# Graph attention and routed experts on one core: a bound on the gathers of the edge pass, and dead edges sent beyond it

## The chip, the cores and the metric

The program runs on one NeuronCore of a Trainium2 chip. The metric is the device time of one execution in microseconds, the median of several. The engines that matter are PE (matrix products), DVE (vector), ACT (scalar functions), POOL (GpSimd, which here makes most of the indirect DMAs) and SP (plain DMAs). Each runs its own instructions in order and waits for the others through semaphores.

## The reference

6250 nodes with 256 features and 100,000 edges, sorted by destination. First a graph attention layer with 8 heads of 32, on layer-normed features, then a layer of 8 experts of which each node takes two; both are added to the residual.

```python
x_l = (x @ W_l + b_l).reshape(n, H, C)
x_r = (x @ W_r + b_r).reshape(n, H, C)
x_j = x_l[src]
g = leaky_relu(x_r[dst] + x_j, 0.2)
alpha = einsum('ehc,hc->eh', g, att) + log(edge_attr)[:, None]
ex = exp(alpha - segment_max(alpha, dst)[dst])
alpha = ex / (segment_sum(ex, dst)[dst] + 1e-16)
out = segment_sum(x_j * alpha[..., None], dst, n).reshape(n, H * C) + bias
...
h = gelu(einsum('td,edh->teh', xf, W1) + b1)
y = einsum('teh,ehd->ted', h, W2) + b2
out = einsum('ted,te->td', y, mask_of_the_two_best_experts)
```

What matters for the change is `x_l[src]`: for every edge, one row of the left table.

## The kernel before

It has four stages. `prepare` norms 49 tiles of 128 nodes and projects them (one tile after another, index `t`), writes the left rows (256 features and 8 numbers for the linear part of the score, 1056 B, the table `left_rows` of 6272 rows) and the right rows to HBM, and builds the lists of the edge pass beside that. `edges` is the edge pass. `route` normalises the sums and chooses experts; `experts` works through 105 tiles of slots, with an indirect DMA of rows in (L1267) and one with addition out (L1657) for each.

Edges are cut into 391 blocks of 256 (`PAIR` = 2 tiles of 128), and each block is worked once for every tile of 128 nodes that its destinations reach. Such a piece of 128 places is an *item*. A block in which a border between two node tiles falls is done twice, as four items instead of two. An edge whose destination lies in the other node tile is dead in that item: its `key` is -1 and its weight is nothing (`-BIG` is added to the logarithm). Each item still gathers all of its 128 left rows, those of dead edges too.

In `prepare`, the edges of the items are gathered on POOL (L332: `rows_d`, `rows_s`, `rows_w`, each with a row of 128 numbers for every item), cast by ACT into `df` (t = 21) and `sf` (t = 24), and DVE makes from them, between the projections of the tiles t = 22 to 26, `local`, `live` and `key` (L657 to L669). At this point an item is a row: partition and the index q of 7 give the item, the last index the edge. From t = 26 PE transposes `local`, `sf` and the logarithms of the weights (L476), one piece of 128 items for each tile, so that the edges lie on the partitions, and ACT copies them out (L532), the sources into `srcs` as whole numbers.

The edge pass runs over 220 groups of four items (878 items and two more). For each group, GpSimd issues four indirect DMAs (L829), one an item, each of 128 rows from `left_rows` into `rows`, by 128 source numbers out of `idx`. `rows` is a ring of 16 groups (`RINGS`): before the first gather of a group, POOL's queue waits for DVE to have weighed the group 15 before it (`weighed`), for the gathers four groups back to have landed, and for the list `idx`, which DVE copies for eight groups at once (L893). PE then sums the right rows (L1191) and the gathered rows (L1193) into `p_row`, ACT rectifies (L1081), DVE scales, adds the linear part and reduces (L909, L914, L924), after every eight groups the maxima are spread and the weights made, and eleven groups later DVE weighs the rows (L1000), PE multiplies by the one-hot destinations (L1254) and DVE adds to the accumulators (L1029). The order on each engine is fixed by the lists of stages and offsets handed to `pipeline`; no instruction order depends on data.

Of the kernel before, what the change touches and what calls it, by code (L numbers as in the profile page):

```python
# [17 lines left out]
ALU = mybir.AluOpType  # L18
# [3 lines left out]
P = 128  # L22
# [16 lines left out]
QI = -(-ITEMS // P)  # L39
# [13 lines left out]
SLOT_TILES = (2 * N + EXPERTS * (P - 1)) // P  # L53
TINY_WEIGHT = 1e-19
SPARE = 704
BY = 7
AHEAD = 8
LEAD = 7
# [4 lines left out]
SENDS = 4  # L63
BATCHES = NODE_TILES // BY
PIECES = ((0, BY), (BY, 4 * BY), (4 * BY, 7 * BY))
PARTS = ((0, 3 * BY), (3 * BY, 6 * BY), (6 * BY, 7 * BY))
EARLY = 3
DL = D + H
NOWHERE = NODE_TILES * P
# [67 lines left out]
def build(nc, x, src, dst, edge_weight, block_ends, W_l, b_l, W_r, b_r, att, bias, Wg, bg, W1, b1, W2, b2, out):  # L137
    with ExitStack() as whole:
# [30 lines left out]
        with ExitStack() as graph:  # L169
# [9 lines left out]
            held("attb", [P, D])  # L179
            held("beside_w2", [P, SPARE])  # L180
            prepare(nc, d, s, x, block_ends, W_l, b_l, W_r, b_r, att, bias)
# [15 lines left out]
def prepare(nc, d, s, x, block_ends, W_l, b_l, W_r, b_r, att, bias):  # L197


    sem = nc.alloc_semaphore  # L200
# [3 lines left out]
    local_done, turned, turned_copied = sem("local_done"), sem("turned"), sem("turned_copied")  # L204
    cleared, weights_in = sem("x_cleared"), sem("p_w_in")
    x_in = [sem(f"x_in{i}") for i in range(len(PIECES))]
    sqrt_ready, sqrt_done, scaled = sem("p_sqrt_ready"), sem("p_sqrt_done"), sem("p_scaled")
    keys_back, floored, logged = sem("keys_back"), sem("weights_floored"), sem("weights_logged")
    local_kept, cast_done, reached_done, found_done, found_kept = sem("local_kept"), sem("cast_done"), sem("reached_done"), sem("found_done"), sem("found_kept")
    const_set, const_ramp, const_masked = sem("const_set"), sem("const_ramp"), sem("const_masked")  # L210
    weights_done, breaks_done, edge_keys_in = sem("weights_done"), sem("breaks_done"), sem("edge_keys_in")
# [7 lines left out]
    with ExitStack() as scope:  # L219
# [30 lines left out]
        sf, df = sb("sf", [P, QI, P]), sb("df", [P, QI, P])  # L250
# [5 lines left out]
        local, live, key = sb("local", [P, QI, P]), sb("live", [P, QI, P]), sb("key", [P, QI, P])  # L256
# [7 lines left out]
        def tiles_of(b):  # L264
            return slice(b * BY, (b + 1) * BY)

# [9 lines left out]
        with nc.Block(no_gpsimd_drain=True) as block:  # L276
# [142 lines left out]
            @block.tensor  # L419
            def _(pe):  # L420
                def turn(t):
                    pe.wait_ge(normed, t + 1)
                    wait(pe, x_turned_copied, t - 1)
                    for h in range(KD):
                        last = nc.tensor.transpose(pt[:, t % 2, h * P:(h + 1) * P], xn[:, t % 2, h * P:(h + 1) * P], s["ident"][:, :])
                    last.then_inc(x_turned, 1)

                def multiply(t):
                    pe.wait_ge(x_turned_copied, t + 1)
                    wait(pe, left_done, t - 1)  # L430
                    wait(pe, right_steps, 2 * (t - 1) - 1)
                    for side, wide in enumerate((DL, D)):
                        for h in range(KD):
                            last = nc.tensor.matmul(py[:, t % 2, side, 0:wide], xT[:, t % 2, h * P:(h + 1) * P],
                                                    W[:, h, side, 0:wide], start=(h == 0), stop=(h == KD - 1))
                    last.then_inc(projected, 1)

                pe.wait_ge(const_ramp, 10)
                turn(0)
                pe.wait_ge(columns_done, 1)  # L440
                pe.wait_ge(weights_in, 64)
                for t in range(NODE_TILES):
                    if t + 1 < NODE_TILES:
                        turn(t + 1)
                    multiply(t)
                    if t == 1:
                        pe.wait_ge(ends_done, 1)
                        for c in range(BLOCK_PARTS):
                            for a in range(2):
                                last = nc.tensor.matmul(ps[0:blocks_in(c), 0, 2 * c + a:2 * c + a + 1], offs[0:1, a, c * P:c * P + blocks_in(c)],  # L450
                                                        s["ones"][0:1, 0:1], start=True, stop=True)
                        last.then_inc(spread, 1)
                    if t == 2:
                        pe.wait_ge(reached_done, BLOCK_PARTS)
                        for c in range(BLOCK_PARTS):
                            last = nc.tensor.matmul(ps[0:2, 0, 0:PAIRS], counted[0:blocks_in(c), c, :], reached[0:blocks_in(c), c, :],
                                                    start=(c == 0), stop=(c == BLOCK_PARTS - 1))
                        last.then_inc(found_done, 1)
                    if t == 3:
                        pe.wait_ge(found_kept, 1)  # L460
                        for q in range(QI):
                            own = found_row[:, q * P // PAIR:(q + 1) * P // PAIR, :].rearrange("a n m -> a (n m)")
                            last = nc.tensor.matmul(ps[:, 1, 2 * q:2 * q + 2], own, s["ident"][0:2, 0:2], start=True, stop=True)
                        last.then_inc(found_done, 1)
                    i = t - 26
                    if 0 <= i < 3 * QI:
                        if i < QI:
                            pe.wait_ge(local_done, 1)
                        else:
                            pe.wait_ge(cast_done, 2)  # L470
                        if i >= 2:
                            pe.wait_ge(turned_copied, i - 1)
                        if i >= 2 * QI:
                            pe.wait_ge(weights_done, 1)
                        from_ = local if i < QI else sf if i < 2 * QI else rows_w
                        nc.tensor.transpose(ps[:, i % 2, 0:P], from_[:, i % QI, :], s["ident"][:, :]).then_inc(turned, 1)  # L476
# [58 lines left out]
            def _(v):  # L535
                step = Chain(v, dve)
# [87 lines left out]
                for t in range(NODE_TILES):  # L624
# [42 lines left out]
                                                            ALU.add, ALU.mult))  # L667
                    if t == 26:
                        nc.vector.tensor_scalar(key[:, :, :], key[:, :, :], -1.0, None, ALU.add).then_inc(local_done, 1)  # L669
                    if t == 28:  # L670
                        v.wait_ge(gathered[2], 16 * QI)
                        step(nc.vector.tensor_scalar(no_weight[:, :, :], rows_w[:, :, :], TINY_WEIGHT, None, ALU.is_lt))
                        nc.vector.tensor_scalar(rows_w[:, :, :], rows_w[:, :, :], TINY_WEIGHT, None, ALU.max).then_inc(floored, 1)
# [53 lines left out]
def edges(nc, d, s):  # L727


    sem = nc.alloc_semaphore  # L730
# [20 lines left out]
    with ExitStack() as scope:  # L751
# [54 lines left out]
        def parity(g):  # L806

            return g.c // TURN % 2
# [3 lines left out]
        with nc.Block(no_gpsimd_drain=True) as block:  # L812
            @block.gpsimd
            def _(pool):
                nc.gpsimd.memset(K[:, :], -BIG).then_inc(cleared, 1)
                nc.gpsimd.memset(unit[:, :], 1.0).then_inc(cleared, 1)

                def gather(g):
                    r = g.slot(RING)
                    goals = ((weighed, g.n - (RINGS - 1)),  # L820
                             (gathered[r], g.turn(RING) * (16 * G)),
                             (listed, g.turn(TURN) + 1))
                    goals = [(m, v if isinstance(v, int) else pool.to_reg(v)) for m, v in goals]
                    pool.wait_ge(cleared, 1)
                    for m, v in goals:
                        wait(pool, m, v)
                    for n in range(G):
                        at = g.c % TURN * G + n
                        nc.gpsimd.indirect_dma_start(  # L829
                            out=rows[:, g.slot(RINGS), n, :], out_offset=None, in_=d["left"][:, :],  # L830
                            in_offset=bass.IndirectOffsetOnAxis(ap=idx[:, parity(g), at:at + 1], axis=0),
                        ).then_inc(gathered[r], 16)

                pipeline(pool, GROUPS, [(0, live(gather))], GROUPS)
                for t in range(EARLY * BY):
                    if t % BY == 0:
                        pool.wait_ge(inverted, t // BY + 1)
                    sums = acc[:, t, :, 0:C]
                    nc.gpsimd.tensor_tensor(sums, sums, inv[:, t, :].unsqueeze(2).to_broadcast([P, H, C]), ALU.mult
                                            ).then_inc(divided, 1)  # L840
                for t in range(EARLY * BY):
                    if t % BY == 0:
                        pool.wait_ge(s["back"][t // BY], 16)
                    pool.wait_ge(divided, t + 1)
                    own = X[:, t, :].rearrange("p (h c) -> p h c", c=C)
                    nc.gpsimd.tensor_tensor(own, own, acc[:, t, :, 0:C], ALU.add).then_inc(rows_added, 1)
# [929 lines left out]
```

## Time and profile before

| | us |
|---|---|
| median of 3 runs | 1837.22 |
| lowest, highest | 1834.57, 1838.47 |
| span of the profiled execution | 1834.0 |

In the page and the rows, busy time is the time in which an engine works on instructions that compute or issue indirect DMAs. Waits name the line that waited, on the left, and who released it, on the right; "issue" means that the profile shows nobody who was waited for. The ends of matmuls are modelled, so PE's busy time is an upper reading. The rows on which the prediction rests stand in a section of their own below.

### The profile page before, as it was taken

What the parts mean: (1) busy time and instruction counts of PE and PEld (TensorE: products, weight loads), DVE (VectorE), ACT (ScalarE), POOL (GpSimd) and SP (SyncE); (2) the same over time, 40 slices, a digit from 0 to 9 for tenths busy, and PEclk for the clock granted to TensorE, in tenths of its full rate; (3) what the DMA queues carried; (4) which work ended last, traced back from release to release, by engine and by line L of the source; (5) the groups of instructions that cost most, each with busy time, mean ns of one, the idle gap of its engine ahead of it and who ended that gap; (6) DMA issues with size and microseconds to landing.
All of it is one profiled execution on the core that took longest, in us unless ns stands there. A gap on an engine that the chain in (4) does not pass through costs nothing. (4 is left out here: it accounts for less than half of the span.)

```text
span 1834.0 us, 36250 instructions
## 1 busy us (share of the span) xinstructions
PE 1704.0 (93%) x9433; PEld 1449.1 (79%) x9434; DVE 1417.0 (77%) x2670; ACT 1250.3 (68%) x3163; POOL 1299.3 (71%) x1358
## 2 busy tenths in 40 slices
PE   6895789999999999999999999998797899999998
PEld 4674578887787888788888888876596799999998
DVE  6774689999999999999999999999868433333333
ACT  3463589999898999999999999987770133233222
POOL 4866777777777777777777777776435677776775
PEclk9997899999999999999999999999857999999999
DMA  6887777877877888777878888774674344444444
GB/s 224 225 267 248 220 235 239 240 242 238 238 243 236 240 241 240 238 244 243 235 245 239 241 241 243 240 236 130 202 244 166 73 78 70 72 71 69 70 73 52
DMA packets 214752, 359.18 MB, mean 196 GB/s; under 512 B 44062, under 2 KB 103880, under 8 KB 214457
## 3 DMA queue, kind: packets, MB, share of 16 engines
q1 hardware_dynamic: 150392, 208.33, 34.9%
q0 software_dynamic: 63072, 147.92, 33.3%
q8 instruction: 63, 1.03, 0.2%
q10 hardware_dynamic: 1120, 1.05, 0.2%
q14 instruction: 105, 0.85, 0.2%
HBM read 302.77 MB, written 54.40 MB: 195 GB/s over the span
## 5 line engine op out<-in xcount | busy, mean ns | idle before, releaser
L829 POOL DMA_INDIRECT rows<-left_rows,idx x880 | 841.1, 956 | 269.3 <-issue 263.9
L1191 PE MATMUL p_row<-rights,hotT 128*128 128x256 f32 x1760 | 504.0, 368 | 55.4 <-issue 26.0
L1193 PE MATMUL p_row<-rows,ident 128*128 128x256 f32 x1760 | 529.8, 383 | 0.0
L1254 PE MATMUL p_gain<-W,hots 128*128 128x264 f32 x1760 | 470.4, 391 | 8.7 <-DVE acc L1029 6.3
L1191 PEld LDWEIGHTS p_row<-rights,hotT 128*128 128x128 f32 x1760 | 322.0, 192 | 131.1 <-issue 82.1
L1254 PEld LDWEIGHTS p_gain<-W,hots 128*128 128x128 f32 x1760 | 324.0, 190 | 78.9 <-issue 24.6
L1081 ACT ACTIVATE L<-p_row 128x512 f32<-128x512 f32 x440 | 259.2, 589 | 127.0 <-PE p_row L1193 125.3
L1708 ACT ACTIVATE e_hT<-e_ph,b_column 128x128 f32<-128x128 f32 x420 | 119.7, 368 | 326.0 <-PE e_ph L1733 326.0
L1000 DVE TENSOR_TENSOR W<-rows,p_weights 128x1024 f32<-128x1024 f32 x220 | 266.9, 1213 | 43.9 <-PE p_gain L1254 41.4
L1151 ACT ACTIVATE far<-iota_row,dl 128x128 f32<-128x128 f32 x880 | 299.2, 391 | 0.0
L909 DVE TENSOR_TENSOR L<-L,p_weights 128x1024 f32<-128x1024 f32 x220 | 266.1, 1210 | 27.0 <-ACT L L1081 27.0
L924 DVE TENSOR_REDUCE raw<-L 128x32 f32<-128x1056 f32 x220 | 272.8, 1240 | 1.4 <-issue 0.2
L1193 PEld LDWEIGHTS p_row<-rows,ident 128*128 128x128 f32 x1760 | 273.7, 191 | 0.0
L1657 POOL DMA_INDIRECT out<-e_y,goes_to x105 | 176.9, 1685 | 87.5 <-DVE e_y L1692 48.9
L1692 DVE TENSOR_TENSOR e_y<-e_py,e_b 128x256 f32<-128x256 f32 x105 | 44.6, 424 | 214.1 <-PE e_py L1744 214.1
L1733 PE MATMUL e_ph<-e_xT,e_w_own 128*128 128x128 f32 x1680 | 206.2, 276 | 0.3 <-DVE e_w_own L1676 0.3
L1744 PE MATMUL e_py<-w,e_hT 128*128 x840 | 198.5, 379 | 0.0
L1733 PEld LDWEIGHTS e_ph<-e_xT,e_w_own 128*128 128x128 f32 x1680 | 197.3, 193 | 0.8 <-issue 0.7
L1029 DVE TENSOR_TENSOR acc<-acc,p_gain 128x264 f32 x440 | 184.6, 420 | 14.3 <-issue 7.5
L1744 PEld LDWEIGHTS e_py<-w,e_hT 128*128 128x128 f32 x840 | 151.6, 190 | 16.3
L1159 ACT ACTIVATE hots<-far,unit 128x512 f32<-128x512 f32 x220 | 158.6, 721 | 6.3
L1089 ACT ACTIVATE apart<-locals,iota_column 128x512 f32<-128x512 bf16 x220 | 155.8, 708 | 2.0 <-DMA locals<-item_locals 1.9
(254 smaller groups left out, 1880.7 us busy)
## 6 DMA issues: line engine op xcount, KB each, us to landing
rights<-right_rows SPq DMA_DIRECT2D x440, 256.0 KB
locals<-item_locals SPq DMA_DIRECT2D x110, 256.0 KB, 3.7
rows<-left_rows,idx POOLq DMA_INDIRECT x880
right_rows<-p_parts SPq DMA_DIRECT2D x49, 256.0 KB
w<-in_L_ffn_W SPq DMA_DIRECT2D x16, 512.0 KB, 6.4
left_rows<-p_y SPq DMA_DIRECT2D x49, 132.0 KB
kept_rows<-X SPq DMA_DIRECT2D x7, 896.0 KB, 4.4
X<-kept_rows SPq DMA_DIRECT2D x7, 896.0 KB, 4.9
```

The source lines that it names most:

```text
L829: nc.gpsimd.indirect_dma_start(out=rows[:, g.slot(RINGS), n, :], out_offset=None, in_=d["left"][:, :], in_offset=bass.IndirectOffsetOnAxis ...
L909: nc.vector.tensor_tensor(own, own, p_weights[:, clear_of, SPAN:SPAN + D].rearrange("p (h c) -> p h c", c=C).unsqueeze(1) .to_broadcast([P ...
L924: nc.vector.tensor_reduce(raw[:, parity(g), :, at:at + 2 * H].rearrange("p u (b h) -> p b u h", h=H), L[:, g.slot(APART), :, :, :].rearran ...
L1000: nc.vector.tensor_tensor(W[:, g.slot(2), :, :, 0:C], rows[:, g.slot(RINGS), :, 0:D].rearrange("p n (h c) -> p n h c", c=C), p_weights[:, ...
L1029: nc.vector.tensor_tensor(to, to, p_gain[:, n, 0:D + H], ALU.add).then_inc(added, 1)
L1081: nc.scalar.activation(L[:, g.slot(APART), PAIR * n:PAIR * (n + 1), :, 0:C].rearrange("p n h c -> p (n h) c"), p_row[:, n, :].rearrange("p ...
L1151: nc.scalar.activation(far[:, n, :], s["iota"][:, :], ACT.Abs, bias=s["dl"][:, bass.ds(g.n * G + n, 1)], scale=-1.0).then_inc(distance, 1)
L1191: nc.tensor.matmul(to, hotT[:, g.slot(2), i, :], rights[:, g.slot(2), n, part * D:(part + 1) * D], start=(part == 0), stop=False)
L1193: last = nc.tensor.matmul(to, s["ident"][:, :], rows[:, g.slot(RINGS), i, 0:D], start=False, stop=True)
L1254: last = nc.tensor.matmul(p_gain[:, n, 0:D + H], hots[:, g.slot(2), i, :], W[:, g.slot(2), i, :, :].rearrange("p h c -> p (h c)"), start=( ...
L1733: last = nc.tensor.matmul(ph[:, g.slot(2), m * P:(m + 1) * P], w1_own[:, g.slot(2), k, m * P:(m + 1) * P], xT[:, g.slot(2), k * P:(k + 1) ...
L1744: last = nc.tensor.matmul(py[:, g.slot(2), 0:D], hT[:, g.slot(2), m * P:(m + 1) * P], w2[:, bass.ds(e, 1), m, :].rearrange("p a f -> p (a ...
```

## The change

Two constants are new: `FULL_ITEMS` = 64 and `ALWAYS` = 16. In `prepare`, after the right rows of tile t = 27, DVE makes for the edges 16 to 127 of every item 6272 (`NOWHERE`, the number of rows in the left table) where the key is below zero and 0 elsewhere, and adds that to the sources `sf`, except for the items 0 to 63. PE's transposes of `sf` wait for that (`sources_skipped`) instead of for the cast. The first 64 items, which are the first to fill the ring `rows`, and the first 16 edges of every item keep their sources. In the edge pass, each gather gets a bound of 6271, and a row whose number is beyond it is left out without an error; its place in `rows` keeps what an earlier group left there. In the built program the bound is in a register, and a register move stands ahead of each gather on POOL's queue (such instructions are left out of the listings below).

```diff
+FULL_ITEMS = 64
+ALWAYS = 16
...
+    skipped = sem("sources_skipped")
...
                         if i < QI:
                             pe.wait_ge(local_done, 1)
                         else:
-                            pe.wait_ge(cast_done, 2)
+                            pe.wait_ge(skipped, 2)
...
+                    if t == 27:
+                        v.wait_ge(local_done, 2)
+                        v.wait_ge(cast_done, 2)
+                        step(nc.vector.tensor_scalar(live[:, :, ALWAYS:P], key[:, :, ALWAYS:P], 0.0, float(NOWHERE), ALU.is_lt, ALU.mult))
+                        nc.vector.tensor_tensor(sf[FULL_ITEMS:P, 0, ALWAYS:P], sf[FULL_ITEMS:P, 0, ALWAYS:P],
+                                                live[FULL_ITEMS:P, 0, ALWAYS:P], ALU.add).then_inc(skipped, 1)
+                        nc.vector.tensor_tensor(sf[:, 1:QI, ALWAYS:P], sf[:, 1:QI, ALWAYS:P], live[:, 1:QI, ALWAYS:P], ALU.add
+                                                ).then_inc(skipped, 1)
...
                         nc.gpsimd.indirect_dma_start(
                             out=rows[:, g.slot(RINGS), n, :], out_offset=None, in_=d["left"][:, :],
                             in_offset=bass.IndirectOffsetOnAxis(ap=idx[:, parity(g), at:at + 1], axis=0),
+                            bounds_check=NOWHERE - 1, oob_is_err=False,
                         ).then_inc(gathered[r], 16)
```

DVE in `prepare`, before, from `key` (t = 26) to the first two instructions on the weights (t = 28):

```order
L669 TENSOR_SCALAR key<-key 128x896
L572 TENSOR_TENSOR p_right<-p_py,p_right_bias 128x256 [waits left_stored3,p_projected]
L576 TENSOR_SCALAR p_parts<-p_right 128x256 [waits p_right_steps]
L572 TENSOR_TENSOR p_right<-p_py,p_right_bias 128x256 [waits left_stored0,p_projected]
L576 TENSOR_SCALAR p_parts<-p_right 128x256 [waits p_right_steps]
L672 TENSOR_SCALAR no_weight<-rows_w 128x896 [waits gathered2]
L673 TENSOR_SCALAR rows_w<-rows_w 128x896 [waits dve_schedule]
```

The same place after (its lines are numbered 3 to 11 higher):

```order
L672 TENSOR_SCALAR key<-key 128x896
L575 TENSOR_TENSOR p_right<-p_py,p_right_bias 128x256 [waits left_stored3,p_projected]
L579 TENSOR_SCALAR p_parts<-p_right 128x256 [waits p_right_steps]
L676 TENSOR_SCALAR live<-key 128x7x112 [waits cast_done,local_done]
L677 TENSOR_TENSOR sf<-sf,live 64x112 [waits dve_schedule]
L679 TENSOR_TENSOR sf<-sf,live 128x6x112
L575 TENSOR_TENSOR p_right<-p_py,p_right_bias 128x256 [waits left_stored0,p_projected]
L579 TENSOR_SCALAR p_parts<-p_right 128x256 [waits p_right_steps]
L683 TENSOR_SCALAR no_weight<-rows_w 128x896 [waits gathered2]
L684 TENSOR_SCALAR rows_w<-rows_w 128x896 [waits dve_schedule]
```

Three instructions are put in behind the right rows of tile 27, and everything behind them on DVE comes later; nothing else moves on any engine.

## Rows read from the trace of the kernel before

**Rows 1.** The page's head and busy time, share of the span, instructions by engine.

```profile
span 1834.0 us, 36250 instructions
PE 1704.0 (93%) x9433; PEld 1449.1 (79%) x9434; DVE 1417.0 (77%) x2670; ACT 1250.3 (68%) x3163; POOL 1299.3 (71%) x1358
```

**Rows 2.** Busy time of each engine between 300 and 1200 us.

```profile
core 0: us, PE busy (x) PEld busy (x) DVE busy (x) ACT busy (x) POOL busy (x), PEclk, DMA share, GB/s
300.00:1200.00 900.00, 877.68 (x4596) 727.62 (x4595) 852.75 (x1347) 823.67 (x1997) 681.48 (x718) 1.00 0.80 240
```

**Rows 3.** Waits between 300 and 1200 us, longest in total first.

```profile
engine line waited for: us in total, times, longest us
POOL rows L829 <- issue: 218.2, 716, 0.3
ACT L L1081 <- PE p_row L1193: 70.1, 176, 1.2
PEld p_row L1191 <- issue: 39.9, 57, 1.8
DVE W L1000 <- PE p_gain L1254: 35.6, 77, 0.9
...
PEld p_turn L1242 <- ACT low L1134: 5.6, 17, 0.3
PE p_row L1191 <- DMA rows<-left_rows,idx: 4.4, 7, 1.4
```

**Rows 4.** POOL in order of time; six gathers of about a group and a half.

```profile
start us, us, engine line op out<-in xcount [idle before <-releaser]
...
691.35 0.94 POOL L829 DMA_INDIRECT rows<-left_rows,idx  x1 [0.30 <-issue]
692.60 0.95 POOL L829 DMA_INDIRECT rows<-left_rows,idx  x1 [0.30 <-issue]
693.85 0.95 POOL L829 DMA_INDIRECT rows<-left_rows,idx  x1 [0.30 <-issue]
695.10 0.94 POOL L829 DMA_INDIRECT rows<-left_rows,idx  x1 [0.30 <-issue]
696.35 0.94 POOL L829 DMA_INDIRECT rows<-left_rows,idx  x1 [0.30 <-issue]
697.59 0.94 POOL L829 DMA_INDIRECT rows<-left_rows,idx  x1 [0.30 <-issue]
```

**Rows 5.** The gathers' line alone: duration, first and last start.

```profile
L829 POOL DMA_INDIRECT rows<-left_rows,idx x880: 942/946/2033, 152.9 to 1260.5; - x176
```

**Rows 6.** Two other indirect DMAs, each line alone, in the same form.

```profile
L332 POOL DMA_INDIRECT rows_w<-in_edge_weight,t_idx x7: 940/944/1128, 48.0 to 71.2; - x7
L1657 POOL DMA_INDIRECT out<-e_y,goes_to x105: 1552/1588/2046, 1443.6 to 1829.8; - x105
```

**Rows 7.** In order of time in `prepare`: DVE around tile 28, and who waits.

```profile
88.48 0.61 DVE L661 TENSOR_SCALAR live<-local 128x896 f32<-128x896 f32 x1
...
94.00 1.15 DVE L669 TENSOR_SCALAR key<-key 128x896 f32<-128x896 f32 x1
...
96.68 0.42 DVE L572 TENSOR_TENSOR p_right<-p_py,p_right_bias 128x256 f32<-128x256 f32 x1 [0.79 <-PE p_py L434]
...
103.86 0.42 DVE L572 TENSOR_TENSOR p_right<-p_py,p_right_bias 128x256 f32<-128x256 f32 x1
...
104.43 1.99 PE L434 MATMUL p_py<-p_W,p_xT 128*128 128x264 f32 x8 [1.21 <-DVE p_right L572]
...
105.47 0.21 ACT L488 ACTIVATE p_std<-p_std 128x7 f32<-128x7 f32 x1 [2.15 <-DVE p_std L550]
...
111.48 0.42 PE L476 MATMUL ps_turn<-ident,sf 128*128 128x128 f32 x1
...
123.49 1.08 DVE L684 TENSOR_TENSOR live<-with_last,key 128x896 f32<-128x896 f32 x1
```

**Rows 8.** The page's queue of GpSimd's DMAs: packets, MB, share.

```profile
q0 software_dynamic: 63072, 147.92, 33.3%
```

**Rows 9.** Lines by cost, and the register operation on DVE's queue.

```profile
L1029 DVE TENSOR_TENSOR acc<-acc,p_gain 128x264 f32 x440 | 184.6, 420 | 14.3 <-issue 7.5 <-PE p_gain L1254 4.0 <-DVE acc L1029 1.3
...
L914 DVE TENSOR_TENSOR L<-rows,logw 128x32 f32<-128x32 f32 x220 | 51.9, 236 | 0.0
...
L1029 DVEq FUSED_REGOPS  x412: 57/57/57, 239.4 to 1315.9; - x138
```

**Rows 10.** The cast of the sources, by its tile.

```profile
L524 ACT ACTIVATE sf<-rows_s x1: 935/935/935, 88.7 to 88.7; 128x896 f32<-128x896 int32 x1
```

## The prediction

> **What bounds the kernel now.** I read the engine totals of the page first, then the edge pass in one window, then who waited for whom in it, then GpSimd alone in order of time. On the page [rows 1] PE looks like the bound: 1704.0 us of 1834.0. The edge pass is most of it. It runs from the first gather at 152.9 us to the last at 1260.5 [rows 5]. In the 900 us from 300 to 1200 [rows 2] PE is busy 877.68 us, DVE 852.75, ACT 823.67, and POOL only 681.48, which reads as if GpSimd had a quarter of its time free. It has not. The list of waits [rows 3] says that POOL's idle time before a gather is "issue", 716 times for 218.2 us and never more than 0.3 us at once. 681.48 + 218.2 is 899.7 of 900 us: GpSimd works without a break, 0.946 us of gather and 0.30 us until the next one can start, 1.25 us in all [rows 4]. 880 gathers at 1.25 us are 1100 us, and the pass lasts 1108.6 us [rows 5]. Four gathers feed one group, so a group takes 5.0 us, whatever the others can do.
>
> The others are close behind. PE's idle share from 300 to 1200 is 22.3 us in 900, or 2.5% [rows 2]; DVE's is 5.3%. So GpSimd sets the pace, and the most that a faster GpSimd could give is about 2.5% of the stretch in which the change acts. That stretch starts behind the first 64 items, which are 16 groups of 5.0 us from 152.9 us, so at 233 us, and ends at 1260: 1027 us, of which 2.5% is 25 us. Behind that PE is the bound. PE's direct waits for gathered rows in this window are only 4.4 us [rows 3]: data that lands earlier, without GpSimd issuing faster, is worth no more than those.
>
> **The parts of the change.** *How many rows are skipped.* There are 391 blocks of 256 edges and 48 borders between node tiles that fall inside a block, so 2 x (391 + 48) = 878 items of 128 places, 112,384 places for 100,096 padded edges. 12,288 places are dead: 256 for each border, spread over the four items there. Without the first 64 items and the first 16 edges of every item, the drawn inputs leave 10,080 skipped places, 9% of all, some 224 for each of 45 borders, and a border comes every 4.5 groups.
>
> *The register.* The bound stands in a register, and the built program has a register move ahead of each of the 880 gathers. I cost it at nothing: the gap between gathers is 0.30 us [rows 4] and never more [rows 3], although every fourth gather stands behind the waits of its group. So the queue works off such instructions while the gather before them is still being made, and the 0.946 us of that gather are the cover. No row of POOL shows a register move in the pass; the nearest is a register operation on DVE's queue, 57 ns [rows 9]. The bounds are thus nothing and, without the cover, 880 x 57 ns, 50 us; I take nothing, by the constant gap. A gain is excluded, as an instruction is only added.
>
> *The gather with a bound, its rows all valid.* No row of before shows one, and this is the term on which all hangs, since GpSimd's time is the stage's time. Below, nothing; a gain on a gather without skipped rows is excluded, as a test is added and no work removed. Above, the costliest indirect DMA of the trace, the scatter with addition: 1.588 us against 0.946 [rows 5, 6], 0.64 us more, which times 880 would be 565 us. I take nothing, by the row that it is nearest to: the seven gathers of the weights also take 0.944 us [rows 6], with 512 B in a row instead of 1056, so the time is that of making 128 descriptors and doesn't react to small differences. I keep a middling price (60 ns) for the rival.
>
> *The skipped rows.* The scatter with addition has to read each of its 128 destinations too, and pays 642 ns for that, 5.0 ns a row [rows 5, 6]. A skipped row needs no descriptor but is still read and compared, so it saves between 0 and 5.0 ns; I take half, 2.5 ns. 10,080 rows at 2.5 ns are 25 us of GpSimd's time (at 5.0 ns 50 us), in steps of 0.56 us every 4.5 groups. PE can use 2.5% of 4.5 x 5.0 us, 0.56 us, in the same time. So saving and headroom are about equal, PE doesn't use all of it (its own waits for DVE and ACT in [rows 3] stay), and I take 20 us. More would not help: with 5.0 ns a row the stage stops at PE's 25 us.
>
> *Traffic.* The skipped rows are 10,080 x 1056 B, 10.6 MB of the 147.9 MB on the GpSimd queue [rows 8], and the DMA engines' share in the pass is 0.80 [rows 2]. Nothing waits there for bandwidth, by the 4.4 us above, so this is worth nothing by itself.
>
> *Three more vector instructions in the preparation.* A tensor_scalar over 784 elements: between the 0.61 us and the 1.15 us that the trace has for 896, so 0.5 to 1.0. A sum over 112 elements of 64 partitions: between 0.236 us for 32 and 0.420 for 264 [rows 9], some 0.25. A sum over 672: 1.08 us for 896 by L684 [rows 7], so 0.8. Together 1.6 to 2.1 us; I take 2.0. They stand behind the 28th tile's right rows. There DVE had 0.79 us idle, then none until 104.28, when PE has been waiting 1.21 us for DVE's right rows [rows 7]. So 2.0 - 0.8 = 1.2 us goes through to PE, and from there to ACT's root and the rest of the preparation, which is on the path. The waits that the new instructions carry are over by then: key ended at 95.15 us [rows 7], the cast of the sources, which began at 88.7, at 89.6 [rows 10]. PE's transposes of the sources wait for them, and come at 111.48, ten microseconds later [rows 7].
>
> **The sum.** 1834.0 (the profiled span) + 1.2 - 20 = 1815.2 us. The median of the runs, 1837.22, is 3.2 us above the profiled span; with that, **1818 us**.
>
> **The rivals.** *A, the forecast: skipped rows make a gather shorter.* For it: the scatter row shows that GpSimd's time does depend on the work per row. Against it: only one other kind shows that, and it is another mode. From 1813 us (PE's 25 us) to 1834; as the ends of matmuls are modelled, PE's true headroom may be larger, and DVE's 5.3% is the farther limit, so I go down to 1808.
>
> *B, nothing in GpSimd's time changes.* A gather takes 0.946 us whether it writes 128 descriptors or 16, since all 128 places are gone through anyway; or the rows are not left out but sent to nowhere, so that the change doesn't do what it says (then the 10.6 MB would still be moved). For it: the gathers' median of 946 ns lies 4 ns above their least of 942 [rows 5], like a fixed price. Time: 1837.2 + 1.2 = 1838 us, with the 4.4 us of waits for landed rows as the only possible gain, so 1834 to 1839. The Trainium skill speaks for this rival: DMA: Bandwidth & Descriptors, "Anatomy of one DMA", calls the generation of descriptors "small, variable", with many descriptors possible before the cost grows. By that rule fewer rows would give nothing. The trace agrees in the constant 0.946 us [rows 5] and disagrees in the scatter's 1.588 us [rows 6].
>
> *C, slower: the test of the bound costs time in every gather.* The place is the loop over 128 indices on GpSimd, which is the bound of the pass; the price is paid 880 times, the skipped rows are only in one gather of seven. Every 10 ns more a gather are 8.8 us. From 23 ns a gather on, A's 20 us are gone; at 60 ns, half a nanosecond a row, it is 53 us: 1838.4 + 52.8 = 1891 us. That is with no saving on skipped rows; with A's it would be 1866 or so. For it: GpSimd has no slack at all [rows 3], and software must compare and count rows which it did not before. Against it: a comparison of 16 or more indices at once would be far below that, and may be made already.
>
> **How the numbers follow.** A 0.44, B 0.20, C 0.36. 0.2% is 3.7 us, about what a measurement of this kernel can tell from no change. A gives faster but for its upper edge (0.42); B and edges of A and C give no difference (0.20); C gives slower, and a little of B with it (0.38). The likeliest case is A, so 1818 us, its own range 1808 to 1834. Signs are mixed, so the whole range reaches into C: 1808 to 1892 leaves out about half of C above (0.16) and a little below. C's far end, 565 us, is in no range; I hold it for unlikely, as it is the price of a second read per row.
>
> **What the profile after would show.** A: the gathers' median stays at 946 ns, but some 128 of them, in runs of two to four every 18, are visibly shorter (a gather with 16 rows left by 0.2 to 0.5 us); POOL shows for the first time waits for DVE's weighing in the pass, and PE's idle share from 300 to 1200 goes from 2.5% towards 1%. B: the same 942 to 946 ns throughout, the last gather at 1261 to 1262 us, queue 0 at 137 MB (or at 148, if nothing is left out). C: the median of all 880 is longer, the last gather comes later by 880 times the difference, and PE and DVE show more idle time. The register move would show as a gap of over 0.30 us with the same 946 ns. The preparation's step shows in the first gather: 154.1 us instead of 152.9. What would make all this wrong is a stage that reacts to stale rows, or a DMA imbalance: skipped rows lie in neighbouring places, so some DMA engines get nothing and others all, and a semaphore that waits for the slowest gains nothing; since landings are not what the pass waits for, I leave it at that.

## The result, and the profile after

The changed kernel takes **1884.5 us** (median; 1883.4 to 1891.0), the kernel before on the same chip 1837.9: 1.026 times as long, 95% interval 1.0246 to 1.0281. It is 47 us slower. The prediction, 1818 us and faster, had the sign wrong; 1884.5 lies inside its whole range, close to where rival C stands. The profiled execution has a span of 1881.7 us, 47.7 more than before. First the head of the page, with the queue of GpSimd's DMAs (packets, MB, share):

```profile
span 1881.7 us, 37134 instructions
PE 1715.0 (91%) x9433; PEld 1454.8 (77%) x9434; DVE 1425.1 (76%) x2673; ACT 1254.4 (67%) x3163; POOL 1346.3 (72%) x1358
...
DMA packets 214758, 348.40 MB, mean 185 GB/s; under 512 B 46610, under 2 KB 106443, under 8 KB 214456
...
q0 software_dynamic: 63072, 137.08, 31.1%
```

Against [rows 1] POOL alone grew by an amount of the size of the loss: 1346.3 us against 1299.3 for the same 1358 instructions. The gathers' line by itself says where (duration as least/median/most in ns, first and last start in us):

```profile
L840 POOLq MOVE  x880: 29/29/29, 153.1 to 1298.2; - x176
L840 POOL DMA_INDIRECT rows<-left_rows,idx x880: 994/998/2086, 153.9 to 1307.6; - x176
its engine sat idle before it (us, times) until:
  issue: 265.6, 871
```

Against [rows 5] a gather takes 998 ns instead of 946. The least rose by the same 52 ns, from 942 to 994, so it is not a few long ones, but each of the 880. 880 x 52 ns are 45.8 us. From first to last gather the pass takes 1153.7 us against 1107.6, 46.1 more, and the span grew by 47.7. In order of time, in the same place as [rows 4]:

```profile
690.93 0.99 POOL L840 DMA_INDIRECT rows<-left_rows,idx  x1 [0.30 <-issue]
692.23 1.00 POOL L840 DMA_INDIRECT rows<-left_rows,idx  x1 [0.30 <-issue]
693.53 1.00 POOL L840 DMA_INDIRECT rows<-left_rows,idx  x1 [0.30 <-issue]
694.83 1.00 POOL L840 DMA_INDIRECT rows<-left_rows,idx  x1 [0.30 <-issue]
```

The gap is still 0.30 us, although 880 register moves of 29 ns now stand on GpSimd's queue. By their starts in the trace, about three in four of them (677) run while a gather is still being made, and the others (203) between two gathers. Starts are 1.30 us apart instead of 1.25. The others gave way, as the window from 300 to 1200 us shows (busy us and instructions of PE, PEld, DVE, ACT and POOL, granted clock, DMA share, GB/s), and its waits:

```profile
300.00:1200.00 900.00, 846.35 (x4417) 700.03 (x4416) 821.98 (x1295) 794.79 (x1918) 690.16 (x689) 1.00 0.75 221
```

```profile
POOL rows L840 <- issue: 210.1, 689, 0.3
ACT L L1093 <- PE p_row L1205: 98.6, 204, 1.4
PEld p_row L1203 <- issue: 79.7, 87, 1.9
PE p_row L1203 <- issue: 48.8, 69, 1.5
```

POOL's 690.16 + 210.1 are again the whole 900 us, as 681.48 + 218.2 were in [rows 2, 3]. PE is busy 31 us less in the same stretch than in [rows 2], and what it idles before is the first instruction of a group: its own weight loads of `p_row` wait 79.7 us instead of 39.9 [rows 3]. The profile names nobody for these waits ("issue"); that they are waits for gathered rows follows from the order of the work and is tested by the experiments. GpSimd still sets the pace, with a slower step.

The skip does happen. Queue 0 moved 137.08 MB instead of 147.92 [rows 8], but in the same 63,072 packets, and by the heads of the two pages 2,548 packets more than before are under 512 B. The sizes of the single packets in the trace tell how: before, all 28,160 packets of the gathers hold four rows of 1056 B; now 25,557 do, 2,549 hold 16 B, that is four pieces of 4 B, and the 54 others are mixtures of the two. So a skipped row is not left out of the transfer, a piece of 4 B stands in its place. Counted this way 10,304 rows are skipped, and 10,304 x 1052 B are the 10.84 MB that are missing.

### The profile page after: what moved, and what is told of

Same layout as the page of the kernel before. It is cut to its first block and busy times, and to the rows that moved or that the text cites. A ratio compares the mean times of both kernels' runs of the same rounds, so it can differ in the third digit from the quotient of the medians.

```text
span 1881.7 us, 37134 instructions
## 1 busy us (share of the span) xinstructions
PE 1715.0 (91%) x9433; PEld 1454.8 (77%) x9434; DVE 1425.1 (76%) x2673; ACT 1254.4 (67%) x3163; POOL 1346.3 (72%) x1358
## 3 DMA queue, kind: packets, MB, share of 16 engines
q0 software_dynamic: 63072, 137.08, 31.1%
## 5 line engine op out<-in xcount | busy, mean ns | idle before, releaser
L840 POOL DMA_INDIRECT rows<-left_rows,idx x880 | 886.7, 1008 | 269.6 <-issue 265.6
```

The costliest lines, as they stand in the source:

```text
L840: nc.gpsimd.indirect_dma_start(out=rows[:, g.slot(RINGS), n, :], out_offset=None, in_=d["left"][:, :], in_offset=bass.IndirectOffsetOnAxis ...
```

## The experiments

The theory after the result: **a bound costs 52 ns on GpSimd in every gather that carries one, whether rows are skipped or not, and a skipped row saves nothing.** The rivals were that the register move costs the time, that the preparation or the skipped places do, or that it isn't GpSimd's time at all that counts. Ratios are to the kernel before, measured beside it on the same chip.

**The bound alone.** The kernel before with the bound, and no source changed:

```
                             in_offset=bass.IndirectOffsetOnAxis(ap=idx[:, parity(g), at:at + 1], axis=0),
+                            bounds_check=NOWHERE - 1, oob_is_err=False,
```

> The kernel before with the bound on every gather and no source moved beyond it, so that nothing is skipped and the preparation is untouched. Theory T (the bound costs some 52 ns in every gather on GpSimd, skipping saves and costs nothing): gathers at a median of 998 ns, last gather about 46 us later than before, 1883 us. Rival D (the skipped rows, which go out as 4-byte descriptors, slow the DMA engines and through them the gathers): 946 ns and 1837 us.

It takes 1884.86 us, ratio 1.0263 [1.0237, 1.0289]: the whole loss, without one skipped row. Its gathers, all 147.92 MB of them moved:

```profile
L829 POOL DMA_INDIRECT rows<-left_rows,idx x880: 994/998/2027, 155.6 to 1308.7; - x176
```

**The preparation alone.** The three vector instructions and their waits stay, but add zero; no bound:

```
-  step(nc.vector.tensor_scalar(live[:, :, ALWAYS:P], key[:, :, ALWAYS:P], 0.0, float(NOWHERE), ALU.is_lt, ALU.mult))
+  step(nc.vector.tensor_scalar(live[:, :, ALWAYS:P], key[:, :, ALWAYS:P], 0.0, 0.0, ALU.is_lt, ALU.mult))
...
-                            bounds_check=NOWHERE - 1, oob_is_err=False,
```

> The changed kernel with its three vector instructions and waits in the preparation, but they add 0 to the sources of dead edges, and the gathers have no bound. Theory T: gathers at 946 ns, first gather at 153.9 us as in the changed kernel (1.0 us later than before), time 1838 us, 1 us above before. If the preparation carried more than its share of the 47 us, it would be well above that.

1837.58 us over ten runs, ratio 0.9999 [0.9988, 1.0009]. The preparation is worth nothing that can be measured, and a gather is as before: 942/949 ns least and median.

**The register set once.** The changed kernel, but the bound's register is written once ahead of the pass, so the 880 moves go:

```
+                bound = pool.to_reg(NOWHERE - 1)
...
-                            bounds_check=NOWHERE - 1, oob_is_err=False,
+                            bounds_check=bound, oob_is_err=False,
```

> The changed kernel with the bound put into one register once, so that the 880 register moves ahead of the gathers go. Theory T: nothing changes, 998 ns a gather and 1884 us, since the moves lie under the gather before them. Rival M (the move is what costs 52 ns): 946 ns and about 1839 us.

1885.26 us, ratio 1.0277 [1.0254, 1.0300], the same as with the moves. The trace has no MOVE row any more, and the gathers read as in the changed kernel:

```profile
L841 POOL DMA_INDIRECT rows<-left_rows,idx x880: 994/998/2136, 152.9 to 1307.7; - x176
```

The moves cost nothing that can be measured, and the rival that the register move costs the time falls.

**The other mode of the bound.** As bound_only, but a row beyond the bound would be reported as an error instead of skipped:

```
-                            bounds_check=NOWHERE - 1, oob_is_err=False,
+                            bounds_check=NOWHERE - 1, oob_is_err=True,
```

(against bound_only)

> As bound_only, but a row beyond the bound would be an error and not skipped (none is beyond it). If it is the comparison with the bound that costs 52 ns: 998 ns a gather and 1883 us, as bound_only. If it is the way of skipping (making a descriptor that moves nothing, for which the code must be ready): 946 ns and 1837 us.

1895.48 us, ratio 1.0326 [1.0307, 1.0345], and a median of 1012 ns:

```profile
L829 POOL DMA_INDIRECT rows<-left_rows,idx x880: 1007/1012/1957, 154.9 to 1319.1; - x176
```

Neither of the two values expected, 998 and 946 ns, came. So it is not skipping alone that costs, but what the two modes do for their 52 and 66 ns, no run here shows. So the price depends on the mode, and skipping is the cheaper of the two. 880 x 14 ns = 12.3 us, against 10.6 us between the two kernels: the time follows the gather's duration once more.

**Half of the gathers with a bound.** The preparation adds zero, and of the four gathers of a group only the first two carry the bound:

```
-                            bounds_check=NOWHERE - 1, oob_is_err=False,
+                            **(dict(bounds_check=NOWHERE - 1, oob_is_err=False) if n < 2 else {}),
```

> The bound on the first two gathers of each group alone (440 of 880), no source beyond it. Theory T (each bounded gather costs 52 ns of GpSimd's time and the pass goes at GpSimd's pace): half of the 47 us, 1837 + 440 x 0.052 = 1860 us; bounded gathers at 998 ns, the others at 946. If the pass had slack that the first bounds use up, it would lie well under 1860; if one bounded gather slowed its neighbours too, above.

1873.92 us, ratio 1.0191 [1.0164, 1.0218]: 14 us more than expected. Half the gathers, half the cost, was too simple. POOL in order of time:

```profile
690.24 0.96 POOL L840 DMA_INDIRECT rows<-left_rows,idx  x1 [0.31 <-issue]
691.50 1.01 POOL L840 DMA_INDIRECT rows<-left_rows,idx  x1 [0.30 <-issue]
692.81 1.01 POOL L840 DMA_INDIRECT rows<-left_rows,idx  x1 [0.30 <-issue]
694.12 0.96 POOL L840 DMA_INDIRECT rows<-left_rows,idx  x1 [0.30 <-issue]
695.38 0.96 POOL L840 DMA_INDIRECT rows<-left_rows,idx  x1 [0.30 <-issue]
```

The two kinds can be told apart one by one: 0.96 without, 1.01 with the bound, so the price sits in the gather that has it. But both kinds are some 10 to 14 ns dearer than where all are alike (0.946 and 0.998). (14 + 62) ns x 440 are 33 us, and the kernel lost 36.6. Why a mixture costs more on both sides is open; I did not test it further.

**Many skipped rows.** The changed kernel, but every place from the 17th on of all items but the first 64 gets the source beyond the table, living edges too. The sums of those edges are left out of what is computed:

```
-  step(nc.vector.tensor_scalar(live[:, :, ALWAYS:P], key[:, :, ALWAYS:P], 0.0, float(NOWHERE), ALU.is_lt, ALU.mult))
+  step(nc.vector.tensor_scalar(live[:, :, ALWAYS:P], key[:, :, ALWAYS:P], 1e9, float(NOWHERE), ALU.is_lt, ALU.mult))
```

> The changed kernel, but every edge from the 17th on of all items but the first 64 is sent beyond the bound, dead or not (so 112 of 128 rows are skipped and most of the sums are left out). Theory T with descriptors made for skipped rows too: 998 ns a gather as before and about 1884 us, with the bytes of the gathers down by 80%. The forecast's step (2.5 ns saved for each skipped row): 112 x 2.5 = 280 ns less a gather, 720 ns, and the pass at the pace of PE, under 1815 us. A rival on traffic (the DMA engines' load slows PE's loads of right rows): a gain of more than 5 us at 998 ns a gather.

1881.27 us, ratio 1.0226 [1.0205, 1.0247]. Nine times as many skipped rows, 91,392 = 816 x 112, and four fifths of the gathers' bytes gone (two thirds of the queue's), and a gather takes what it took:

```profile
L840 POOL DMA_INDIRECT rows<-left_rows,idx x880: 994/998/2196, 155.2 to 1309.0; - x176
...
q0 software_dynamic: 63072, 51.78, 15.5%
...
300.00:1200.00 900.00, 847.63 (x4415) 697.61 (x4414) 823.36 (x1294) 796.13 (x1917) 690.24 (x689) 1.00 0.48 141
```

998 ns again, still 63,072 packets, and PE no busier (847.63 us) although the DMA engines' share fell from 0.75 to 0.48. A skipped row saves nothing on GpSimd that the trace, which shows whole nanoseconds a gather, could show. Nor does the traffic count in the pass: from first to last gather it takes 1153.8 us, against 1153.7 in the changed kernel. The loss against the kernel before is smaller than the changed kernel's, by 3 us in the medians and by 7 us in the ratios; the two intervals just overlap, so whether something outside the pass gained a few microseconds is open.

**What the others can take.** Without a bound, the fourth gather of each group is left out from the 17th group on; its 128 places keep older rows, so a quarter of the sums is left out of what is computed, while PE, DVE and ACT do all their work:

```
-                    for n in range(G):
+                    for n in range(G if g.n < RINGS else G - 1):
```

(and the waits count three landings for such a group)

> The kernel before without the fourth gather of each group from the 17th group on (the fourth item of a group then works on rows of an earlier group, so a quarter of the gathered rows is left out). GpSimd needs 3 x 1.25 = 3.75 us a group. If GpSimd sets the pace of 5.0 us and PE comes right behind it, as the forecast said, the pass is at PE's pace: 25 us less, 1812 us. If another engine or a chain of them sets 5.0 us too, less than 5 us are gained. If PE's modelled ends hide idle time and DVE's 5.3% is the limit, up to 54 us.

1814.26 us, ratio 0.9863 [0.9837, 0.9890]. With a quarter of GpSimd's work gone the kernel gains 23 us, and no more:

```profile
300.00:1200.00 900.00, 897.40 (x4701) 743.57 (x4700) 867.37 (x1376) 838.33 (x2042) 520.31 (x551) 1.00 0.73 218
```

PE is busy 897.40 of 900 us. This is the ceiling that the prediction read off as 25 us.

**The bound where GpSimd is not the pace.** three_gathers with the bound on every gather (the same sums left out):

```
+                            bounds_check=NOWHERE - 1, oob_is_err=False,
```

> As three_gathers with the bound on every gather, nothing beyond it. GpSimd needs 3 x 1.30 = 3.9 us a group, still below the 4.9 us of PE. Theory T: the bound costs 52 ns in each of the 676 gathers, but only the 16 full groups at the start are paced by them: 64 x 0.052 = 3 us above three_gathers at most. If the bound hurt in another way than through GpSimd's pace (landings, DMA), some 35 us above it.

1816.30 us, 2.0 us more than three_gathers, with gathers of 998 instead of 946 ns:

```profile
L833 POOL DMA_INDIRECT rows<-left_rows,idx x676: 992/998/2259, 153.5 to 1235.5; - x169
```

The same 52 ns are there 676 times, 35 us, and nearly all of it lies beside PE's work. What is left is no more than the runs of one kernel differ by, and fits the first 64 gathers, where all four are still made: 64 x 52 ns = 3.3 us.

**Fewer rows instead of skipped rows.** What would a row save that is not asked for at all? From the 17th group on each gather gets 64 partitions instead of 128; the sums of the other half of the places are left out of what is computed:

```
+                        own = P if g.n < RINGS else P // 2
                         nc.gpsimd.indirect_dma_start(
-                            out=rows[:, g.slot(RINGS), n, :], out_offset=None, in_=d["left"][:, :],
-                            in_offset=bass.IndirectOffsetOnAxis(ap=idx[:, parity(g), at:at + 1], axis=0),
+                            out=rows[0:own, g.slot(RINGS), n, :], out_offset=None, in_=d["left"][:, :],
+                            in_offset=bass.IndirectOffsetOnAxis(ap=idx[0:own, parity(g), at:at + 1], axis=0),
```

> The kernel before, without a bound; from the 17th group on each of the four gathers of a group fetches rows for its first 64 partitions only (the other 64 places keep the rows of an earlier group, so the sums of those edges are left out of what is computed). It asks whether a gather's 0.946 us on GpSimd belongs to the instruction or to its rows. Theory 'by the row': a gather of 64 rows takes about 473 ns, the 816 of them fall to 0.473 + 0.305 = 0.78 us, a group to 3.1 us, and PE sets the pace: about 1814 us, as in three_gathers. Theory 'a fixed part': 400 to 900 ns, and the part that doesn't halve is what every gather pays; theory 'fixed altogether': 946 ns and 1837 us. I hold a mixture for likely, 500 to 650 ns, with the time near 1814.

> half_rows with the bound on every gather, all rows valid (the same sums left out). It asks whether the 52 ns that a bound costs in a gather of 128 rows belong to the instruction or to its rows. Theory 'a test for each row': 26 ns more than half_rows has for its 64 rows. Theory 'a fixed price of the other path': 52 ns more. In time the difference is small, since PE sets the pace here: 1814 to 1818 us. I expect 26 ns, since a bound that reports an error cost another 14 ns, which looks like work per row.

That first pair fell on a chip whose granted clock was 0.88 in these runs, where the kernel before took 2318 us, half_rows 2335 and half_rows_bound 2368; its times say nothing, and only GpSimd's durations were read: 902 ns and, with the bound, 937. The 500 to 650 ns held for likely were far off; what came is the upper end of "a fixed part". Both again:

> half_rows once more, for its time at an undisturbed clock (in the first run TensorE's granted clock was 0.88 and the kernel before took 2318 us, so that only the durations on GpSimd could be read). From the 17th group on a gather fetches 64 rows; the sums of the other 64 places are left out. In the first run a gather took 0.946 us with 128 rows and 0.902 with 64: 0.34 ns a row. Theory 'nearly all of a gather's time is paid once for the instruction': 816 gathers x 44 ns = 36 us less on GpSimd, more than the 23 us that the other engines leave, so 1814 to 1818 us, with PE as the bound, as in three_gathers. A rival, 'it is the traffic and the landing that count, not GpSimd': half of the pass's gathered bytes are gone, so clearly under 1810.

> half_rows_bound once more, for its time at an undisturbed clock (same sums left out). In the first run, gathers with a bound took 0.998 us with 128 rows and 0.937 with 64. 0.937 + 0.305 is 1.242 us a gather, 4.97 us a group, against the kernel before's 5.00: GpSimd is hardly faster than in the kernel before and sets the pace. Theory 'GpSimd's time is the time of the pass': 816 x 9 ns = 7 us less than before, and the first 64 gathers 3 us more, so about 1833 us. Rival 'the bound costs nothing once the rows are few': as half_rows, 1814 to 1818 us.

(44 ns for 64 rows are 0.69 ns a row; the 0.34 ns in the expectation divided by 128. The sum in it goes by the 44 ns and stands.) half_rows_b takes 1811.72 us, ratio 0.9860 [0.9831, 0.9889], half_rows_bound_b 1833.81, ratio 0.9987 [0.9974, 1.0000]. Their gathers, first without the bound up to 236 us (128 rows) and from 239 us on (64 rows, but for the first two):

```profile
L830 POOL DMA_INDIRECT rows<-left_rows,idx x60: 942/947/2277, 156.4 to 235.3; - x60
...
L830 POOL DMA_INDIRECT rows<-left_rows,idx x818: 892/901/1302, 239.0 to 1240.9; - x164
```

then with it:

```profile
L830 POOL DMA_INDIRECT rows<-left_rows,idx x59: 994/998/2158, 154.8 to 235.3; - x59
...
L830 POOL DMA_INDIRECT rows<-left_rows,idx x819: 932/937/1376, 239.2 to 1259.1; - x164
```

Halving the rows takes 46 ns off a gather of 947. If that is linear (an estimate from these two points), a row costs 0.7 ns and an instruction some 855 ns whatever its rows. The bound adds 51 ns at 128 rows and 36 ns at 64, so by the same estimate about 0.23 ns a row and some 21 ns a gather; the expectation of 26 ns, "by the row", was too low. Half the gathers' rows gone gave 25 us, about as much as three_gathers, with PE again at its limit in the window:

```profile
300.00:1200.00 900.00, 896.85 (x4701) 744.02 (x4700) 868.29 (x1376) 838.98 (x2042) 661.95 (x734) 1.00 0.65 191
```

With PE at its limit this run alone can't refute the rival that landing and bytes count. Its partner does: half_rows_bound_b moves as few bytes and takes back all but 3 us of the gain, as expected (1833). With 9 ns a gather less than the kernel before, GpSimd is the pace again, 679.82 + 219.9 us of 900, and PE has idle time again:

```profile
300.00:1200.00 900.00, 883.85 (x4632) 733.43 (x4631) 858.72 (x1360) 828.71 (x2013) 679.82 (x723) 1.00 0.64 188
POOL rows L830 <- issue: 219.9, 721, 0.5
```

So all kernels of this list read alike: where GpSimd sets the pace, the time follows the number of gathers times their duration; where it doesn't, the time stands at 1812 to 1816 us.

No version here beats the kernel before with all its sums computed. Fewer gathers with more than 128 rows each would save GpSimd most of its time, if the estimate of 855 ns carries beyond 128 rows, but the kernel could gain no more than the 23 to 25 us up to PE's limit; this was not tried.

## Why the prediction failed

The forecast of the span was 1815.2 us and 1881.7 was measured, 66.5 us more: 45.8 for the bound that was put at nothing, 20 for the saving that did not come, and 0.7 that is less than the runs differ by.

*What bounds the kernel: right.* GpSimd without a break, four gathers a group, is shown by the time's following the gather's duration in bound_only, bound_err and half_rows_bound_b. The headroom of 25 us behind it measured 23 (three_gathers) and 25 (half_rows_b).

*The register: right.* 880 moves of 29 ns appear, most of them under a gather as the text said, the gap stays at 0.30 us, and one_register without them is no faster.

*The gather with a bound, its rows all valid: wrong, and this is the step that turned the sign.* The text took nothing between bounds of 0 and 565 us, "by the row that it is nearest to": the gathers of the weights, with rows of 512 B, take the same 0.944 us. That row shows that the bytes of a row don't matter. It says nothing of work added to a gather, and a bound is that. Measured: 52 ns, 45.8 us in all. It is little beside the scatter's 642 ns, yet more than twice the break-even of 23 ns that rival C named. With a term of which the sign of the whole hangs, and no row that shows it, the zero end of its bounds was the choice that favoured the forecast.

*The skipped rows: wrong.* The text took 2.5 ns a skipped row by dividing the scatter's extra 642 ns by 128 rows. sixteen_rows shows nothing saved, 998 ns with 112 of 128 rows skipped, and "a skipped row needs no descriptor" does not fit its packets, where a piece of 4 B stands for each skipped row. But even a row that is truly not asked for saves only some 0.7 ns (half_rows_b), 7 us for all 10,304. The division was the fault: the scatter is another mode, as the text itself objected, no run shows what its 642 ns are for, and two different operations don't give the price of a row. Two sizes of one operation would have, and the kernel before has none.

*How many rows are skipped.* 10,304, not 10,080: 46 borders of 224, one more than counted. Nothing hangs on it.

*Traffic: right for the pass.* With 96 MB fewer in sixteen_rows it lasts 1153.8 us instead of 1153.7.

*The preparation.* In order of time, after shows the three new instructions on DVE and PE's wait for DVE's right rows behind them:

```profile
97.29 1.34 DVE L676 TENSOR_SCALAR live<-key 128x784 f32<-128x784 f32 x1
98.67 0.57 DVE L677 TENSOR_TENSOR sf<-sf,live 64x112 f32<-64x112 f32 x1
99.27 1.27 DVE L679 TENSOR_TENSOR sf<-sf,live 128x672 f32<-128x672 f32 x1
...
107.63 3.46 PE L437 MATMUL p_py<-p_W,p_xT 128*128 128x264 f32 x8 [1.97 <-DVE p_right L575]
```

They took 3.2 us, not the 2.0 of the sum, and each was longer than the bounds given for it. PE's wait is 1.97 us instead of 1.21 [rows 7], 0.8 us more where 1.2 were foreseen, and where the text's own rule would give 3.2 - 0.8 = 2.4. So that 0.8 lies near 1.2 is luck: the sum was too small and the rule let too much through. The first gather starts at 153.9 us, foreseen 154.1, but that confirms nothing: without any of these instructions it starts at 155.6 in bound_only and 156.4 in half_rows_b, with them at 152.9 in one_register. By prep_only's interval the whole preparation costs at most 0.1%, so 1.2 us is neither shown nor refuted.

*The rivals.* B was right that a skipped row changes nothing on GpSimd. It leaned on a line of the Trainium skill (DMA: Bandwidth & Descriptors, "Anatomy of one DMA"): descriptor generation is "small, variable", and many descriptors can be emitted before the incremental cost shows. The 0.7 ns a row of half_rows_b agree with that; "small" does not fit gathers that hold GpSimd for 946 ns, some 855 of them fixed by the estimate, and so bound the stage. C was the case: without a saving it gave 1838.4 + 880 x its price; with the measured 52 ns in place of the 60 that is 1884.2 us, and the chip says 1884.5. Its mechanism, place and sum stood; its chance was too low. That its 60 ns lie so near the 52 is luck, as no row stood behind them, and its "loop over 128 indices" is shown in part alone: by the two sizes some 30 of the 52 ns go with the rows.

## What to carry to other kernels

Before a test, a mode or a skip is put into an instruction that the bounding engine issues many times, multiply its count by what one more test may cost, here a few tens of nanoseconds: 880 gathers turned 52 ns into 46 us, and nothing that the test avoids downstream counts as long as that engine sets the pace. A row that is skipped by its bound is not a row less: only fewer instructions, or, by far less, fewer partitions in one, shorten GpSimd's part here, and by the estimate from two sizes some 855 of a gather's 946 ns belong to the instruction. How much of that the kernel gets is set by the next engine, here 23 to 25 us up to PE's limit. And a term on which the sign hangs should be measured at two sizes of the same operation, not taken from another kind of operation.

## What the runs showed of the hardware

- A gather of 128 rows by indirect DMA holds GpSimd 946 ns, one of 64 rows 901 ns; with a bound 998 and 937; with a bound that reports errors 1012 (128 rows). Rows of 512 B and of 1056 B cost alike [rows 5, 6].
- By the sizes of the packets, each skipped row is still there as a piece of 4 B: 63,072 packets whether 0, 10,304 or 91,392 rows are skipped.
- A register move ahead of a gather takes 29 ns and costs nothing that can be measured: 677 of 880 run while a gather is still being made, and the gap between two gathers is 0.30 us with them and without.
- Gathers mixed, two with a bound and then two without, are each 10 to 14 ns dearer than where all are alike. The cause is open.
